# Two gated cross-attention layers with mixtures of experts: how an expert's last part is run, and when token rows are gathered

## The reference

```python
x = x + tanh(g_xattn[0]) * L0_xattn(layernorm(x), ctx_1024, ...)   # x: 4 x 512 x 256
x = x + tanh(g_ffn[0])   * L0_ffn(layernorm(x), router_w, up_w, down_w)
x = x + tanh(g_xattn[1]) * L1_xattn(layernorm(x), ctx_1024, ...)
x = x + tanh(g_ffn[1])   * L1_ffn(layernorm(x), gate_w, gate_b, w1, b1, w2, b2)
```

## Time and profile before

| | |
|---|---|
| median of 3 runs | 1387.7 us |
| the profiled execution | 1375.1 us, of it the span of instructions 1372.7 us |
| granted clock of PE, mean | 0.990 |
| PE busy | 1311.3 us (96%), 9798 products |
| DVE, ACT, POOL busy | 780.5, 737.5, 480.3 us |
| down products (L434) | 3 x 896; up products 3 x 640 on `m_xt` tiles and the rest on `turned` tiles |
| gathers (L2629), adds (L2649) | 208 and 112 indirect DMAs |
| expert stages | about 418 to 838 us and 1108 to 1362 us |

### The profile page before, as it was taken

The page is one execution under the profiler, slowest core; times in us unless marked ns, Lnnn a source line. Parts: engine busy times, 40 slices in busy tenths (PEclk is TensorE's granted clock), DMA queues, the critical chain, the costliest instruction groups (busy, mean ns, idle before and its releaser), DMA issues. The chain is left out here.

```text
span 1372.7 us, 25408 instructions
## 1 busy us (share of the span) xinstructions
PE 1311.3 (96%) x9798; PEld 1232.0 (90%) x9798; DVE 780.5 (57%) x1736; ACT 737.5 (54%) x1405; POOL 480.3 (35%) x378
## 2 busy tenths in 40 slices
PE   6999999999989999999999998999999889999996
PEld 5987969969659999999999998899999779999996
DVE  6567687785874535535435334576777865457322
ACT  4455565554555556655555554455553645656644
POOL 0101001000026646556566543110201256767533
PEclk9999999999999999999999999999999999999998
DMA  6102041230235536445353334031212275564322
GB/s 226 63 13 93 16 130 47 68 93 1 95 108 140 149 57 158 114 90 147 84 127 64 57 63 120 0 111 66 83 36 93 78 233 134 138 169 111 53 46 41
DMA packets 73675, 127.48 MB, mean 93 GB/s; under 512 B 7952, under 2 KB 53664, under 8 KB 73504
## 3 DMA queue, kind: packets, MB, share of 16 engines
q1 hardware_dynamic: 46816, 81.92, 18.1%
q0 software_dynamic: 26688, 43.34, 16.7%
HBM read 100.44 MB, written 24.79 MB: 91 GB/s over the span
## 5 line engine op out<-in xcount | busy, mean ns | idle before, releaser
L2555 DVE TENSOR_TENSOR m_hidden_lo<-m_act_out,m_hidden_hi 128x512 fp32r<-128x512 f32 x224 | 154.8, 692 | 349.2 <-ACT m_hidden_hi L2495 338.3
L434 PE MATMUL banks<-m_down_hi,m_hidden_hi 128*128 128x256 f32 x896 | 256.2, 286 | 0.4 <-DVE lists L1674 0.4
L434 PE MATMUL banks<-m_down_lo,m_hidden_hi 128*128 128x256 f32 x896 | 253.7, 283 | 0.0
L434 PE MATMUL banks<-m_down_hi,m_hidden_lo 128*128 128x256 f32 x896 | 253.7, 283 | 0.0
L434 PE MATMUL banks<-m_xt_hi,m_up_hi 128*128 128x256 f32 x640 | 184.1, 288 | 1.4 <-DVE m_xt_lo L2538 1.4
L434 PE MATMUL banks<-m_xt_hi,m_up_lo 128*128 128x256 f32 x640 | 180.7, 282 | 0.0
L434 PE MATMUL banks<-m_xt_lo,m_up_hi 128*128 128x256 f32 x640 | 180.6, 282 | 0.0
L434 PEld LDWEIGHTS banks<-m_down_hi,m_hidden_hi 128*128 128x128 f32 x896 | 169.9, 190 | 3.1 <-DVE lists L1674 0.5
L434 PEld LDWEIGHTS banks<-m_down_lo,m_hidden_hi 128*128 128x128 f32 x896 | 169.8, 190 | 0.0
L434 PEld LDWEIGHTS banks<-m_down_hi,m_hidden_lo 128*128 128x128 f32 x896 | 169.7, 189 | 0.0
L2495 ACT ACTIVATE m_hidden_hi<-m_act_out 128x512 fp32r<-128x512 f32 x224 | 141.6, 632 | 7.1
(11 more groups left out here) (387 smaller groups left out, 3426.9 us busy)
## 6 DMA issues: line engine op xcount, KB each, us to landing
stage<-in_up SPq DMA_DIRECT2D x22, 512.0 KB, 5.4
stage<-in_down SPq DMA_DIRECT2D x21, 512.0 KB, 4.1
stage<-in_ctx_rows SPq DMA_DIRECT2D x20, 512.0 KB, 3.9
stage<-in_ctx_cols SPq DMA_DIRECT2D x24, 402.0 KB, 3.8
m_stage<-in_down SPq DMA_DIRECT2D x10, 512.0 KB, 5.4
m_stage<-in_up SPq DMA_DIRECT2D x9, 512.0 KB, 5.3
rows<-xn SPq DMA_DIRECT2D x8, 528.0 KB, 3.4
stage<-in_ctx_picked SPq DMA_DIRECT2D x8, 512.0 KB, 4.5
```

Source lines behind the costliest of these rows:

```text
L434: mm = q.e.matmul(dst, a, b, start=first and n == 0, stop=last and n == 2, skip_group_check=True)
L2555: q.e.tensor_tensor(lo, m.act[(n * HP + h) % ACTS], f32(hi), ALU.subtract).then_inc(*hidden_lo.mark((layer, n, h)))
```

## The change

Five edits. (1) An end that `HALVES` names for its layer is entered with up to 128 tokens more than its blocks hold. It runs the downs of the last block up to f = 3, then branches: with no tokens left to the rest of the downs ("whole"), otherwise to the rest of the downs and then a half block, `tensor_half`: the ups of the next part on its first 128 tokens only, and its downs for one group of 128 tokens. The half makes no transposes. The other engines run the part as before, at full width. (2) An end raises the left-out semaphores at f = 4 in place of f = 0. (3) The way from an end to `after` is a conditional branch that is always taken, with a hint set at the beginning of the end, of its whole or of its half. (4) No branch lies between parts 5, 6 and 7 on any engine, and `ENDS` is put in another order. (5) POOL gathers part j+2 in block (e, j), where it gathered part j+3; part 3 of an expert is gathered in block 1 in place of the opening, and in layer 1 the gather of (1, 0) goes ahead of that of (0, 2).

```diff
@@ -45,7 +45,11 @@
 EARLY = (3, 2)
-ENDS = ((7, 6, 1, 2, 3, 5, 4), (7, 6, 5, 4, 1, 3, 2))
+PARTS = 5
+
+ENDS = ((1, 2, 5, 3, 4), (5, 4, 3, 1, 2))
+
+HALVES = ((3, 4), (1, 2, 3, 4))
 _COLS = [
     ("bv_s", KD), ("bv_c", KD), ("bg", KD), ("sides", 2),
@@ -103,6 +107,10 @@
         if self.parts is not None:
             self.parts.switch_bb(name, parent=self.top)
+
+    def far_branch_always(self):
+
+        return self.e.mark_branch_hint_location()
     def far_branch(self, held, most):
@@ -2312,13 +2320,15 @@
         def further(q, layer, held, own, e, j, block, finish):
-            if j == NB:
-                either(q, layer, j, finish)
-                return
             before_, passed = [s.count for s in own], dict(q.passed)
             with q.e.If(held > BLOCK * j):
                 block(q, layer, e, j)
-                further(q, layer, held, own, e, j + 1, block, finish)
+                if j < PARTS:
+                    further(q, layer, held, own, e, j + 1, block, finish)
+                else:
+                    for rest in range(PARTS + 1, NB):
+                        block(q, layer, e, rest)
+                    either(q, layer, NB, finish)
             with q.e.Else():
                 catch_up(q, own, before_)
                 either(q, layer, j, finish)
@@ -2337,8 +2347,9 @@
         up_ring = Ring([ps[:, i, :] for i in range(5)])
         y_bank = ps[:, 6, :]
-
-        def tensor_down(q, layer, n, e, f, left_out=None):
+        up_emptied = {}
+
+        def tensor_down(q, layer, n, e, f, left_out=None, tiles=BT):
             m = exp[layer]
             d, (h_hi, h_lo) = m.downs[e % 2], m.hidden[f // 2]
             q.wait_ge(*ready(quarter(layer, e, KD + f // 4)))
@@ -2349,13 +2360,13 @@
                 q.wait_ge(*route_dve.of("put", layer, BATCH - 1, TT - 1))
             if layer and f == 0:
                 q.wait_ge(*set_up.of("own"))
-                for i in range(BT):
+                for i in range(tiles):
                     q.e.matmul(y_bank[:, i * D:(i + 1) * D], m.own[:, e, :], b2, start=i == 0, stop=False, skip_group_check=True)
-            for i in range(BT):
+            for i in range(tiles):
                 c = slice((f % 2) * BLOCK + i * P, (f % 2) * BLOCK + (i + 1) * P)
                 mm = three(q, y_bank[:, i * D:(i + 1) * D], (h_hi[:, c], h_lo[:, c]), (d[0][:, f, :], d[1][:, f, :]),
                            f == 0 and i == 0 and layer == 0, f == HT - 1)
-                if f == 0 and left_out and left_out[i]:
+                if f == HT // 2 and left_out and left_out[i]:
                     mm.then_inc((up_done, turned_block)[i].sem, left_out[i])
             if f % 2 and left_out is None:
@@ -2379,6 +2390,7 @@
                 up_ring.from_first()
             for h in pairs:
                 bank, emptied = up_ring.take((layer, n, h), activated, (layer, n, h))
+                up_emptied[layer, n, h] = emptied
                 for k in range(KD):
                     q.wait_ge(*ready(quarter(layer, e, k)))
                 q.wait_ge(*block_lo.of(layer, n))
@@ -2403,35 +2415,78 @@
                     tensor_down(q, layer, n - 1, e, f)
             tensor_ups(q, layer, e, j, range(HP))
-        def tensor_end(q, layer, e, j, before_):
-
-            up, turned, down = [s.count - c for s, c in zip((up_done, turned_block, down_done), before_)]
+        def tensor_half(q, layer, e, j, up, turned, down):
+
+            n, xt, u = numbered(e, j), block_xt(layer, e, j), exp[layer].ups[e % 2]
+            for h in range(HP):
+                bank = up_ring.of((layer, n, h))
+                q.wait_ge(*block_lo.of(layer, n))
+                q.wait_ge(*up_emptied.get((layer, n, h), (up_done.sem, 0)))
+                for f in (2 * h, 2 * h + 1):
+                    fs, part = slice(f * P, (f + 1) * P), bank[:, (f % 2) * BLOCK:(f % 2) * BLOCK + P]
+                    for k in range(KD):
+                        mm = three(q, part, (u[0][:, k, fs], u[1][:, k, fs]), (xt[0][:, k, 0:P], xt[1][:, k, 0:P]),
+                                   f % 2 + k == 0, k == KD - 1)
+                    if f == 0 and turned:
+                        mm.then_inc(turned_block.sem, turned)
+                mm.then_inc(up_done.sem, 1 + (up - HP if h == HP - 1 else 0))
             for f in range(HT):
-                tensor_down(q, layer, numbered(e, j) - 1, e, f, (up, turned, down - HP))
+                tensor_down(q, layer, n, e, f, (0, 0, down), 1)
+
+        def tensor_leave(q, layer, e, held, name, told):
+
+            q.e.br_cmp(q.e.to_reg(held), BATCH * TOK, on_true=f"after_{layer}_{e}", on_false=f"stay_{name}",
+                       comp_op="IS_LE").branch_hint(told)
+            q.go_on_at(f"stay_{name}")
+            q.e.br(f"after_{layer}_{e}")
         def tensor_expert(q, layer, e):
             own, at = [up_done, turned_block, down_done], {}
             held = count_of(q, layer, e)
             for j in range(always(e), NB):
-                if j + 1 < NB:
-                    told = q.far_branch(held, BLOCK * (j + 1))
+                most = BLOCK * (j + 1) + (P if j + 1 in HALVES[layer] else 0)
+                if j + 1 <= PARTS:
+                    told = q.far_branch(held, most)
                 tensor_block(q, layer, e, j)
-                if j + 1 < NB:
+                if j + 1 <= PARTS:
                     at[j + 1] = [s.count for s in own], dict(q.passed)
-                    q.e.br_cmp(q.e.to_reg(held), BLOCK * (j + 1), on_true=f"end_{layer}_{e}_{j + 1}",
+                    q.e.br_cmp(q.e.to_reg(held), most, on_true=f"end_{layer}_{e}_{j + 1}",
                                on_false=f"block_{layer}_{e}_{j + 1}", comp_op="IS_LE").branch_hint(told)
                     q.go_on_at(f"block_{layer}_{e}_{j + 1}")
             for f in range(HT):
                 tensor_down(q, layer, numbered(e, NB - 1), e, f)
             q.e.br(f"after_{layer}_{e}")
-            for j in ENDS[layer]:
-                if j in at:
-                    q.go_on_at(f"end_{layer}_{e}_{j}")
-                    before_, q.passed = at[j][0], dict(at[j][1])
-                    tensor_end(q, layer, e, j, before_)
-                    q.e.br(f"after_{layer}_{e}")
-            q.passed = dict(at[always(e) + 1][1])
+            left = {j: [s.count - c for s, c in zip(own, before_)] for j, (before_, _) in at.items()}
+            first = dict(at[always(e) + 1][1])
+            ends = [j for j in ENDS[layer] if j in at]
+            for j in ends:
+                up, turned, down = left[j]
+                halved, last = j in HALVES[layer], j == ends[-1]
+                q.go_on_at(f"end_{layer}_{e}_{j}")
+                q.passed = dict(at[j][1])
+                told = None if halved else q.far_branch_always()
+                for f in range(HT // 2):
+                    tensor_down(q, layer, numbered(e, j) - 1, e, f, (0, 0, 0))
+                if halved:
+                    q.e.br_cmp(q.e.to_reg(held), BLOCK * j, on_true=f"half_{layer}_{e}_{j}", on_false=f"whole_{layer}_{e}_{j}",
+                               comp_op="IS_GT")
+                    q.go_on_at(f"whole_{layer}_{e}_{j}")
+                    told = q.far_branch_always()
+                passed = dict(q.passed)
+                for f in range(HT // 2, HT):
+                    tensor_down(q, layer, numbered(e, j) - 1, e, f, (up, turned, down - HP))
+                tensor_leave(q, layer, e, held, f"{layer}_{e}_{j}", told)
+                if halved:
+                    q.go_on_at(f"half_{layer}_{e}_{j}")
+                    q.passed = passed
+                    told = None if last else q.far_branch_always()
+                    for f in range(HT // 2, HT):
+                        tensor_down(q, layer, numbered(e, j) - 1, e, f, (0, 0, 0))
+                    tensor_half(q, layer, e, j, up, turned, down - 2 * HP)
+                    if not last:
+                        tensor_leave(q, layer, e, held, f"{layer}_{e}_{j}_half", told)
+            q.passed = first
             q.go_on_at(f"after_{layer}_{e}")
         def tensor_experts(q, layer):
@@ -2664,31 +2719,31 @@
             if j == 0:
                 gpsimd_opening(q, layer, e)
                 return
-            if 1 < j < NB - 2:
-                gpsimd_there(q, layer, e, j + 2)
+            if 1 < j < NB - 1:
+                gpsimd_there(q, layer, e, j + 1)
             gpsimd_add(q, layer, e, j)
             if (e, j) == (0, 1):
-                gpsimd_there(q, layer, 0, 3)
+                if layer == 0:
+                    gpsimd_gather(q, layer, 0, 3)
                 gpsimd_gather(q, layer, 1, 1)
                 gpsimd_gather(q, layer, 2, 0)
-            if j + 3 < NB:
-                gpsimd_gather(q, layer, e, j + 3)
+                if layer:
+                    gpsimd_gather(q, layer, 0, 3)
+            elif j + 2 < NB:
+                gpsimd_gather(q, layer, e, j + 2)
         def gpsimd_opening(q, layer, e):
             n = numbered(e, 0)
```

(10 more changed lines are left out.)

## The result

The changed kernel took **1374.4 us** (median of ten runs, 1371.9 to 1383.9), the kernel before 1384.7 us (ten runs, 1379.3 to 1389.6) beside it on the same chip. The ratio is 0.9934, 95% interval 0.9911 to 0.9956: 9 us faster (10 by the medians), inside the range and with the right sign, but less than half of the forecast 23.3 us; by the prediction's own 1% this is no change, to which it gave a chance of 0.20.

A forecast was written before the change was run, and what follows sets the result against it. PE's products were taken to bound both expert stages. Terms of -19.8 (halves), +1.1 (last half), -3.7 (gap) and -0.9 (gathers) gave -23.3 us, from 1387.7 to 1364.4 us, range 1350 to 1382.

The forecast's parts named there:

- Which experts: Expert stages: 6 of 56 blocks are halved, layer 0's experts 2, 6, 7 and layer 1's 1, 2, 6.
- a half on PE: PE at ends: narrow products 0.111 us each, halves of 8.5 and 9.2 us, 3.3 us saved each, 19.8 for six.
- (B): Rival for PE's halves: 128-column float32r products run at 0.22 us, as plain float32 does; 1393 us, chance 0.09.
- (A): Rival at the ends: ACT or POOL is late, so a half saves 2 us, not 3.3; 1372 us, chance 0.13.
- The branches: PE's jumps at ends: hinted far and short unhinted ones cost nothing, and layer 1's expert 6 loses its gap; -3.7 us.
- The gap goes: PE's leave of layer 1's expert 6: the 2.5 us gap and 1.2 us of low clock vanish, -3.7 us.
- (C): Rival at leaves of ends: hints are worth nothing, seven more leaves cost 3.7 us each; 1394 us, chance 0.07.
- Layer 0's last half: Start of attention 1, behind layer 0's expert 7: PE comes early and waits for a_x_in, +1.1 us.
- The gathers: POOL's gathers: one pair fewer per expert under six parts; a 0.93 us wait in layer 1 goes, -0.9 us.
- The swap of (1,0) and (0,2): Start of layer 1: the first wait becomes 4.2 us, the next shrinks as much; sum zero, between -2 and +3.5.
- (D): Rival for POOL: gathers one block later come too late, a few stalls, +5 to +10 us, 1370 to 1374; chance 0.08.
- The later signals: Ends raise left-out counts 2.9 us later for POOL and ACT; zero cost, at most 2.9 us of ACT per whole end.

The follow-up runs named there:

- after_again: The changed kernel, unchanged, profiled on another execution; 1379.4 us in its one run.
- after_more: The changed kernel, unchanged, run again on the chip of other runs; 1373.5 us, 0.9968 of the kernel before.
- no_halves: The changed kernel with HALVES empty, so no expert takes a half and ends are 48 products; 1380.9 us, 0.9955 of the kernel before.
- plain_leave: The changed kernel with a plain, unhinted branch from each end to the code behind the expert; 1396.2 us, 1.0060 of the kernel before.
- no_half_more: The changed kernel, but layer 0's expert 7 takes a whole part in place of a half; 1373.3 us, 0.9972 of the kernel before.
- both: The changed kernel without the half of layer 0's expert 7, and with (0,2) gathered ahead of (1,0) in layer 1; 1369.2 us (0.9864), repeated 1370.5 (0.9936).
- gathers_only: The kernel before with nothing but the change of POOL's gathers; 1379.2 us, 0.9933 of the kernel before.
- gathers_more: The kernel before with POOL's changed gathers alone, run again on another chip; 1375.8 us, 0.9986 of the kernel before.
- gathers_before: The changed kernel with all of POOL's gathers as in the kernel before; 1384.2 us, 0.9980 of the kernel before.
- series 4: One of five series of runs, each with its own runs of the kernel before on the same chip; that kernel's median here was 1378.5 us.
- half_07_pad: The changed kernel without the half of layer 0's expert 7, plus 397 never-executed PE instructions that move layer 1's code back; 1378.4 us, 0.9999 of the kernel before.

## Why the prediction was off

**Which experts, and a half on PE: right.** Six halves, 8.5 and 9.2 us each, narrow products at 0.111 us. (B) is dead, and (A) too: in the profile of after there is no wait for the chain beyond 0.34 us in a half (0.90 and 0.43 us in one half of after_again).

**The branches: the step that failed.** "So a hinted far jump is free at 96 products' lead and a short unhinted one too; I cost both at nothing" and "The gap goes", -3.7 us. The gaps of after cost 5.7 us in layer 0 and 8.3 in layer 1, against 2.5 before, plus the clock of 0.60 and 0.55 behind the last. That is +11.5 for the forecast's -3.7, some 15 us of the 19.8 that the halves should bring (13 and 15 by the profiles of after_again and after_more). Two things were missed. The absence of gaps in the kernel before was read as a property of hints; its leaves were short jumps, and the halves turned ends of 48 products into ends of 144 that the leaves now have to pass; with short ends (no_halves) no leave of layer 0 has a gap and the long one of layer 1 is 0.45 us. And whether a hinted leave costs 0.5 or 4 us depends on where the code lies: 397 unused instructions brought the gap ahead of expert 7 back from 0.52 to 3.70 us. (C) had the right mechanism, missed leaves, but not the size: hinted ones mostly cost 0.5 to 0.9 us, and (C)'s 3.7 us each came with plain_leave (0.4 to 6.1), which was slower than before as (C) had it. That the gaps are a fetch of code is an explanation that no run here shows directly.

The Trainium skill ("Runtime: NRT & Kernel Launch", Instruction fetch mechanics) has a taken branch out of the pages held stall for a fetch. The traces agree for unhinted branches (2.6 and 6.1 us in plain_leave), and the dependence on the code's place fits code held in pages; which page is held when, no run here shows.

**Layer 0's last half: mis-sized.** Forecast +1.1 us, found +3.6 in attention 1, so this half gives nothing. The wait was about what I charged (1.44 us for `a_x_in`; my own times, 840.6 and 839.1, made 1.5, not 1.1); what I left out is the clock. Windows of PE from 4 to 20 us behind the stage's start, one later in it, and the whole stage, after:
```profile
840.52:844.52 4.00, 2.23 (x8) 0.57 0.51 55
844.52:848.52 4.00, 3.37 (x8) 0.50 0.47 128
848.52:856.52 8.00, 7.29 (x32) 0.82 0.92 343
...
1066.52:1078.52 12.00, 11.12 (x70) 0.72 0.21 35
836.52:1106.40 269.88, 256.22 (x1815) 0.96 0.24 75
```
and no_half_more:
```profile
842.44:846.44 4.00, 1.72 (x7) 0.92 0.44 54
846.44:850.44 4.00, 3.99 (x14) 0.65 1.00 364
850.44:858.44 8.00, 6.84 (x42) 1.00 0.57 212
...
1068.44:1080.44 12.00, 10.26 (x90) 1.00 0.42 89
838.44:1102.56 264.12, 248.15 (x1816) 0.99 0.24 76
```
With the half the clock is near 0.5 for both first windows and 0.82 in the third, without it 0.92, 0.65 and 1.00. The fourth rows lie 230 us behind the stage's start: there too the clock falls with the half and not without, and over the whole stage it is 0.96 against 0.99. These two profiles are far apart; the five with half 7 have 0.96 to 0.97, the twelve without it 0.97 to 0.99, and the longer attention 1 is, the lower its clock. So the stage's length goes with the clock. The missing share of the clock, summed over time, is 3.8 us in the first 20 us with half 7 and 2.4 without (means), and 6.5 against 2.4 us in the rest of the stage: most of the difference lies late in the stage, not behind the wait for `a_x_in`. What links half 7 to the late falls, which some kernels without it have too (both, 0.97), is open.

**The gathers: mis-sized the other way.** Forecast -0.9 us; gathers_only and gathers_more gave -8.6 and -2.7 us against the kernel before of their series, gathers_before +6 (by ratios, across series). I had read the waits for DVE's low part from one profile with a single one of 0.93 us. The second has 2.69, 0.45, 0.39 and 0.65 in layer 1, and three under 0.7 in layer 0. That the edit gives what these waits cost, and gives more where the kernel before is late more often, is my reading and not shown: no profile of gathers_only has the 8.6 us. Against it stands the 1.6 us of the longer DRAIN at the end, which these figures already contain. The swap of (1,0) and (0,2) came as told: a wait of 2.7 to 4.4 us at the first place, none for DMA at the second. (D) did not happen: no wait for a gather in layer 0.

**The later signals** cost nothing that can be told, as predicted.

**The sum again:** -23.3, +15 for the branches, +2.5 for half 7, between -1.8 and -7.7 for the gathers, is -7 to -13 us against the measured -9.1 and, in series 4, -5.0. This sum takes the gaps from one profile and is no proof to the last us. Layer 1's stage alone differed by 8.8 us between two profiles of one kernel (gathers_only 264.5, gathers_more 255.7). And part of the layer 1 loss is not in the halves at all but in where the code lies, by up to 5 us (258.5 against 253.2; 255.8 with the pad).

**Open:** why a hinted leave misses at one place of the code and not at another; why the small gaps of layer 0 move between executions of the same kernel; and why the kernel before, alone of those run twice or more, differs by 11 us between series.

The best version is both (1370.5 us where the changed kernel had 1373.5 and the kernel before 1378.5; 0.9936 and 0.9864 in two series): the change without half 7, with the old order of the first gathers.

## What to carry to other kernels

Work taken off the bounding engine in blocks of runtime-chosen code is worth what is left after the jumps: count how many instructions each taken branch now passes, and price hinted far jumps at 0.5 to 1 us, not at zero, with some at 3 to 4. A gain right before a stage whose first input comes from another chain becomes a wait, and the granted clock can fall behind it: here the stage behind took 3.6 us more for a wait of 1.4. Before a stall in one profile is priced, take a second profile of the same kernel.

## What was not expected of the hardware

Code that is never executed changed the time by 5.0 us (half_07_pad, 1378.4 against 1373.3 us), and the gap ahead of one branch target from 0.52 to 3.70 us. The kernel with two hinted branches behind a block took 1384.5 us where that with one took 1370.5, with gaps of 1.2 to 3.0 us at the targets of either; with one they were 0 to 1.2 us in layer 0 and up to 1.6 us in layer 1. The same change of gathers made POOL's last DRAIN 4.97 us in place of 3.34 in each of the profiles that has it. A product of 128 columns starts 0.111 us behind the last one as one of 16 columns does, where one of 256 takes 0.121. Halving the columns of 48 ups saved 0.5 us of a half's 3.4; the rest came from 24 downs and the transposes that are left out.
